# A transformer block on one core: the load of the first slot tile moved one unit ahead, slot transpositions put first in a unit's first tick

## What is computed

```python
x = L0_attn_x
xn = _layernorm(x, axis=-1)
x = x + _L0_attn_ref(xn, ...) + _L0_ffn_ref(xn, ...)
```

## Time and profile before

| | us |
|---|---|
| median of 3 runs | 1902.03 |
| lowest and highest of them | 1900.02, 1903.42 |
| the profiled execution, its own time | 1901.16 |
| its span, first to last instruction | 1899.4 |
| PE busy within the span | 1852.7 (98%) |
| DVE, ACT, POOL busy | 1404.4, 1227.9, 1004.9 |
| mean granted TensorE clock, share of full speed | 0.994 |

### The profile page before, as it was taken

One profiled execution on the slowest core, in us unless ns is written; L12 is line 12 of the kernel. 1 busy time (PEld: TensorE's weight loads), 2 busy tenths in 40 slices (PEclk: granted clock), 3 DMA queues, 4 the chain that ended last, 5 costly groups with the idle time before them and its releaser, 6 DMA issues.

```text
span 1899.4 us, 53283 instructions
## 1 busy us (share of the span) xinstructions
PE 1852.7 (98%) x20422; PEld 1682.9 (89%) x20422; DVE 1404.4 (74%) x4092; ACT 1227.9 (65%) x3354; POOL 1004.9 (53%) x1506
## 2 busy tenths in 40 slices
PE   5899999999999999999999999999999999999998
PEld 2489899999999998999999999999999898989987
DVE  7688887777777776776676677667667788887886
ACT  4566666666666766666666666666666666666664
POOL 0244447677867663343433443443342867676774
PEclk9999999999999999999999999999999999999999
DMA  9545302434343413445446445445452232323322
GB/s 269 207 180 184 123 24 86 133 115 148 101 149 115 137 65 103 142 158 190 151 141 199 147 150 183 165 144 177 162 168 68 61 120 85 116 73 98 91 74 62
DMA packets 158602, 249.91 MB, mean 132 GB/s; under 512 B 27280, under 2 KB 112528, under 8 KB 158352
## 3 DMA queue, kind: packets, MB, share of 16 engines
q1 hardware_dynamic: 134688, 150.79, 24.2%
q0 software_dynamic: 23664, 95.70, 15.7%
HBM read 151.54 MB, written 94.90 MB: 130 GB/s over the span
## 4 chain that ended last, share of the span: by engine, by line
PE 94%; issue 0%; DVE 0%; ACT 0%; POOL 0%; DMA 0%; POOLq 0%; DVEq 0%; SPq 0%
PE d_bank L695 20%; PE d_bank L747 16%; PE d_bank L733 13%; PE d_bank L722 12%; PE d_bank L763 9%; PE d_bank L708 9%; PE d_bank L821 6%; PE d_bank L808 3%; PE d_bank L779 2%; PE d_bank L831 1%; PE d_bank L768 1%; PE d_bank L790 0%; POOL d_probs L1343 0%; ACT d_probs L890 0%; DMA d_x<-queued_rows 0%
## 5 line engine op out<-in xcount | busy, mean ns | idle before, releaser
L1343 POOL TENSOR_SCALAR d_probs<-d_probs,d_inverse 128x512 f32<-128x512 f32 (+3 forms) x1024 | 553.4, 557 | 695.4 <-DVE d_inverse L1023 692.2
L890 ACT ACTIVATE d_probs<-d_probs,d_bias 128x512 f32<-128x512 f32 (+3 forms) x1024 | 562.8, 553 | 159.6 <-DVE d_bias L1017 159.6
L1017 DVE CUSTOM_DVE_ANT_0 d_probs<-d_bank,mask 128x512 f32<-128x512 f32 (+3 forms) x1024 | 430.1, 485 | 1.9 <-PE d_bank L733 1.9
L695 PE MATMUL d_bank<-d_xnt,wqk_all 128*128 128x512 f32 x1536 | 408.8, 401 | 0.6 <-PEq L146 0.6
L695 PEld LDWEIGHTS d_bank<-d_xnt,wqk_all 128*128 128x128 f32 x1536 | 271.2, 188 | 52.2 <-issue 0.6
L747 PE MATMUL d_bank<-d_probs_t,d_v 128*64 128x128 f32 x5120 | 309.1, 276 | 0.0
L747 PEld LDWEIGHTS d_bank<-d_probs_t,d_v 128*64 128x64 f32 x5120 | 278.2, 137 | 16.8 <-issue 5.0
L733 PE MATMUL d_bank<-d_ks,d_qs 64*128 64x512 f32 (+3 forms) x3072 | 274.4, 324 | 8.9 <-issue 7.1
L733 PEld LDWEIGHTS d_bank<-d_ks,d_qs 64*128 64x128 f32 x3072 | 242.5, 187 | 25.2 <-issue 9.0
L722 PEld LDWEIGHTS d_bank<-ident_r,d_probs_moved 64*128 64x128 f32 x5120 | 221.2, 135 | 26.0 <-issue 26.0
L722 PE MATMUL d_bank<-ident_r,d_probs_moved 64*128 64x64 f32 x5120 | 235.6, 245 | 3.6 <-POOL d_probs L1343 3.5
(11 more groups left out here) (126 smaller groups left out, 2167.8 us busy)
## 6 DMA issues: line engine op xcount, KB each, us to landing
queued_rows<-d_zeros SPq DMA_DIRECT2D x79, 256.0 KB, 2.4
d_x<-queued_rows SPq DMA_DIRECT2D x79, 256.0 KB, 3.9
routed_rows<-d_y SPq DMA_DIRECT2D x79, 256.0 KB, 2.7
expert_rows<-d_w SPq DMA_DIRECT2D x32, 384.0 KB, 3.0
a_x_in<-in_L_attn_x SPq DMA_DIRECT2D x16, 512.0 KB, 7.9
xn_rows<-a_xn SPq DMA_DIRECT2D x16, 512.0 KB, 4.9
d_normal<-xn_rows SPq DMA_DIRECT2D x32, 256.0 KB, 3.2
d_base<-in_L_attn_x SPq DMA_DIRECT2D x32, 256.0 KB, 3.5
```

The costliest lines, as they stand in the source:

```text
L695: last = pe.matmul(to[:, :], wqk[:, n % PAIRS, "qk".index(kind), wa, k, :], xnt[n // PAIRS % 2][:, xb, k, :], start=first, stop=(k == KD - ...
L890: act.activation(part, part, ACT.Exp, bias=bias[:, i, h:h + 1], scale=-1.0, accum_out=total[which][:, at % 4:at % 4 + 1]).then_inc(exp_don ...
L1017: dve.tensor_tensor_reduce(out=probs[:, i, h, 0:cols], in0=bank(f"s{fill}", u, h)[:, at * P:at * P + cols], in1=mask[:, T - cols:T], scale ...
L1343: pool.tensor_scalar(part, part, inverse[which][:, at % 4:at % 4 + 1], 1.0, ALU.mult, ALU.mult).then_inc(norm_done, 1)
```

## The change

The change does three things, and nothing else is altered:

- load_slots(0) is issued on SP in slot 0 of unit 51 instead of slot 1 of unit 52. load_slots(1) stays where it was.
- In a part 0, PE does xt first, then dn, then gu, instead of dn, gu, xt; tick() lists the stages in that order, so that the banks go with it. Part 1 keeps its order.
- ACT's split_xt also waits for gu_ready of the tile before, since PE's order no longer says that gu has read xt. On ACT the same count of gu_ready is waited for by slot_gate, which stands ahead of split_xt in the same tick.

```diff
--- before.py
+++ after.py
@@ -483,7 +483,8 @@
             n = TICKS.get((u, part))
             if n is None:
                 return {}
-            return {kind: n - back for kind, back in (("dn", 2), ("gu", 1), ("xt", 0)) if 0 <= n - back < SLOT_TILES}
+            stages = (("dn", 2), ("gu", 1), ("xt", 0)) if part else (("xt", 0), ("dn", 2), ("gu", 1))
+            return {kind: n - back for kind, back in stages if 0 <= n - back < SLOT_TILES}
 
         def order(u):
 
@@ -660,9 +661,9 @@
                             load_normal(b + 1, slot - 2)
 
                         n = TICKS.get((u, slot // 2))
+                        if u == FIRST_TICK - 1 and slot == 0:
+                            load_slots(0)
                         if n is not None and slot % 2:
-                            if n == 0:
-                                load_slots(0)
                             if n + 1 < SLOT_TILES:
                                 load_slots(n + 1)
                         n = TICKS.get((u, 0)) if slot == 2 else TICKS.get((u - 1, 1)) if slot == 0 else None
@@ -834,11 +835,13 @@
 
                 def ticks(u, part):
                     n = tick(u, part)
+                    if "xt" in n and not part:
+                        slot_transposes(n["xt"])
                     if "dn" in n:
                         slot_down(n["dn"])
                     if "gu" in n:
                         slot_expand(n["gu"])
-                    if "xt" in n:
+                    if "xt" in n and part:
                         slot_transposes(n["xt"])
 
                 for u in STEPS:
@@ -942,6 +945,8 @@
 
                 def split_xt(t):
                     act.wait_ge(xt_ready, t + 1)
+                    if t:
+                        act.wait_ge(gu_ready, t)
                     act.activation(xt[:, HI, :, :].rearrange("p k n -> p (k n)"), bank("xt", t)[:, :], ACT.Copy
                                    ).then_inc(xt_hi, 1)
```

## The result

The changed kernel takes 1896.04 us (median of 10, 1892.62 to 1901.09), against 1901.76 for the kernel before (1899.18 to 1904.58): ratio 0.9974, 95% interval 0.9965 to 0.9983. The ratio is an estimate from all executions; the two medians alone give 0.9970, that is 5.7 us less. Forecast were 1896.3 and 5.7 us. The profiled execution took 1896.01 us, its span, from the first to the last instruction, 1894.3. What follows shows that the sum came out right while two of its parts did not.

A forecast was written before the change was run, and what follows sets the result against it. PE, busy 1852.7 of 1899.4 us, was taken as the bound. 2.5 (wait) + 1.55 (clock) + 1.6 (order) = 5.7 us gained, giving 1896.3 us against the median 1902.03; range 1893.0 to 1899.5.

The forecast's parts named there:

- Term 1: Unit 52: PE's wait of 2.51 us for the load of d_x goes entirely, with the load issued in unit 51.
- Term 2: Unit 52: K and V behind the wait on d_x no longer run at a lowered clock; 1.55 us gained.
- Term 3: Part 0 of 39 ticks: the new order of groups on PE saves 0.04 us a tick, 1.6 us in all.
- Sum 3.98, against 4.02: Part 0 of a tick: forecast us for xt, dn, gu and K in the new order, against the old order.
- The border behind the scores: Part 0: the first group behind the scores pays a surcharge, 0.11 us on dn; xt there forecast at 0.36 us.
- rival 1: Part 0: the order gives nothing, xt bears the whole surcharge behind the scores; gain 4.1 us, time 1897.9; chance 0.20.
- What costs nothing: Slot loads for a part 0: 10.5 us from issue to need, against a longest landing of 7.8 us.
- The second rival: From tick 1 PE waits again, or the load lands late, or the clock falls; about 1899 to 1900.4; chance 0.08.
- the whole is wrong: Sign: a new PE wait in a part 0, at L822 or L832, or a clock below 1.00 in the expert ticks.
- The banks and ACT's added wait: Part 0: gu starts 1.3 us after DVE's read of the scores; ACT's wait adds at most one instruction passing at once.

The follow-up runs named there:

- the second trace: The kernel before, unaltered, profiled once more; its stretch from unit 52's scores to the K projection behind the last tick took 700.6 us.
- the load alone: The changed kernel with only the load of tile 0 moved, PE keeping dn, gu, xt in part 0: 1899.75 us, ratio 0.9985.
- the second measurement: The changed kernel measured again with nothing altered: 1896.84 us, ratio 0.9977 against the kernel before.
- the order alone: The changed kernel with the load of tile 0 back in unit 52, so only part 0's order (with banks and ACT's wait) changed: 1899.54 us, ratio 0.9985.

## Why the prediction was right, point by point

- **Term 1, the wait**: right. It was there in every trace with the load in unit 52 (1.86 to 2.79 us) and in none with the load in unit 51.
- **Term 2, the clock**: right in size (1.55 forecast; 1.5 in the second trace), and with term 1 exactly the 4.1 us of the load alone. Wrong in that I took it for certain: one of four waits had no fall behind it.
- **Term 3, the order**: direction right, size wrong. "Sum 3.98, against 4.02" holds within 0.01 for the four groups it names (measured 3.99 in unit 53). But they explain the smaller part of the gain. The step that failed is that the sum ended with K. V, Q and the output projection behind it each gain 0.02 to 0.04 us, and the term is 4.0 us, not 1.6. I had read V as 1.41 and Q as 1.40 in unit 53 without asking what they are in a unit without a tick.
- **The border behind the scores**: xt takes 0.37 there, neither the 0.40 of rival 1 nor the 0.29 of its old place. Rival 1, no gain from the order, is refuted. The Trainium skill (TensorEngine Tiling (Array Packing), Key Properties) states that changing the tiling mode drains TensorE. The trace agrees in that the first group behind the scores pays something, 0.08 us on xt as 0.11 on dn. The rule says nothing of the groups further behind, where 2.9 us of the gain were.
- **"What costs nothing", the slot loads**: wrong. I compared 10.5 us in unit 53 with the longest landing of one trace, 7.8 us. The tightest units leave 8.9 to 9.0 us, and six other traces show landings of 10.0 to 10.3 us, one of them that of the kernel before. The second rival's "the load lands late after all" is what happened, in other units than I meant: 0.8 to 1.2 us given back where it was profiled. A new wait on a load at L832 was also the prediction's own sign that "the whole is wrong"; by this sign it failed, though the loss was smaller than the gain that it had left out.
- **The banks and ACT's added wait**: right, no cost.
- **The total**: 5.7 forecast, 5.7 between the medians; the second measurement gives 5.1 (1901.97 and 1896.84). In the profiled executions the stretch holds 4.1 + 4.0 - 0.8 = 7.3 us, and 2.3 us are lost outside it, most of them where the clock fell more often. So the hit is in part luck: an underestimated gain, an unforeseen loss, and a gain in the stretch that the execution times show only in part.

## What to carry to other kernels

Where one engine is full, compare orders by the time from group start to group start, and follow the comparison down the row until the times are the same again: a short group of transpositions went with four slower groups behind it, not one. The slack of a transfer has to be read in the tightest of its repetitions, and its landing in more than one trace. A load moved ahead of others on a shared queue can move the collision to the next transfer; move it out of the crowd, or move the crowd.

## What the runs showed of the hardware that was not expected

- V, 12 matmuls of 256 columns, takes 1.41 to 1.42 us when gu, four transpositions and K stand ahead of it, and 1.37 to 1.39 when the transpositions stand ahead of gu or gu is not there, though a whole K projection lies between. Why the slower rhythm carries so far is open; no experiment here isolates it.
- The granted clock fell behind pauses of 1.86, 2.51 and 2.79 us and not behind one of 2.04 us, so the length of a pause does not settle it.
- The load of tile 0, 256 KB, issued at the same place, landed after 4.3, 3.6 and 3.8 us in three traces (before, before again, the order alone), and after 5.6 us where it was issued 1.0 us sooner. Slot loads in the crowded unit took up to 10.3 us, against medians of 3.4 to 3.9; behind the one of 9.5 us the DMA engines were 94% busy over 5 us.
